# A fill and a wait on GpSimd after every gather of an edge-convolution kernel

## The chip, the cores and the metric

One core of a Trainium2 chip runs the whole kernel. The metric is the device time of one execution in microseconds. Three runs of the kernel before took 2430.92, 2434.01 and 2440.19 us; the median is 2434.01 us.

## The reference

A graph has 6250 nodes with 64 features and 200,000 edges, sorted by their destination. What is computed, cut to what matters:

```
xn   = batch-normalised x (over the nodes, gamma, beta)
feat = concat(xn[dst], xn[src] - xn[dst])          # 200000 x 128
h    = relu(feat @ W1 + b1)                        # 200000 x 128
msg  = h @ W2 + b2                                 # 200000 x 64
agg  = segment_max(msg, dst, 6250), 0 where a node has no edge
out  = layernorm(x + relu(agg))                    # over the 64 features
```

## The kernel before

The first layer is split: one part of it depends on the destination node alone, the other on the source node alone. So the kernel first makes two tables in DRAM, `a_dram` (destination part) and `b_dram` (source part, one row of 128 floats for every node). The edges are cut into two halves (h = 0, 1) and these into windows; the main loop runs over 196 steps (`NI`), k = 0 to 195, each with four tiles of 128 edges from either half, 1024 edges in all.

A step gets the source part of its edges in one of three ways.

- 28 steps (`picked`, every seventh) take it by matmuls with one-hot tiles: DVE makes the one-hot tiles (line 919, `oh`), PE multiplies them (lines 1146 and 1153, `ps_g`). This work is spread over all steps.
- The first 12 gathered steps (`gather(g)`, line 494) have rows of `x` fetched, 64 floats each, into `xs`, a view of `xb`.
- The other 156 (`gather_wide(i)`, line 511) have rows of `b_dram` fetched into `xb[:, u]`, one of eight buffers (`NXB`). PE transposes them straight into the hidden layer's bank (line 1205, `rows_wide`).

A gather is one indirect DMA that POOL issues: its index column `src_ix[:, b, q + t, h:h + 1]` names 128 rows, one for every partition. A step takes 8 gathers (4 tiles, 2 halves; the very first step takes 4). There are 92 narrow and 1248 wide ones, 1340 in all.

POOL's program is in order and short: it makes constants (lines 478 to 486), issues the 12 narrow groups, loads a flag, waits until `b_dram` is written, issues the 156 wide groups, and at the end scatters the last rows of the output (line 526). What paces it in the wide groups is the reuse of the eight buffers. Group i from 8 on waits until PE has transposed group i - 8:

```
                if i >= NXB:
                    pool.wait_ge(wide_ps, i - NXB + 1)
                elif i >= NXB - NX // 2:
                    pool.wait_ge(x_ps, 2 * u + 2)
```

On the other side PE waits in `rows_wide` on `wide_in[u]`, which the landed gathers raise. Nothing else waits for POOL in the main loop. In each step PE does, in order: the transposes of the running maxima of step k - 2 (`turn`, line 1196), the hidden layer of step k (lines 1205 and 1215), the messages of step k - 1 (line 1190), the node sums of step k - 2 (line 1234) and its share of one-hot matmuls. ACT takes `ps_mr` and the hidden layer out of PSUM (lines 683, 688) and makes the window's one-hot rows (lines 640, 644). DVE makes the pick masks (line 972), scans the messages (line 993) and makes `oh`. Once in seven windows DVE and ACT also do a layer norm (lines 923 to 954). SP loads keys, resets, tables and node windows on a queue of its own.

Of the kernel before, what the change touches and what calls it, by code (L numbers as in the profile page):

```python
# [6 lines left out]
def edge_conv_program(nc, x, src, dst, gamma, beta, W1, b1, W2, b2, out):  # L7
# [13 lines left out]
    P = 128  # L21
    N, C = x.shape
# [65 lines left out]
    def wide_slot(i):  # L88
        return (i + NX // 2) % NXB
# [4 lines left out]
    def sides(k):  # L94
        return 1 if k == 0 else 2

    def landed(g):
        return 16 * TG * sides(gathered[g])
# [11 lines left out]
    with ctx:  # L110
        def sb(name, shape, dt=f32):
            return ctx.enter_context(nc.sbuf_tensor(name, shape, dt))
# [4 lines left out]
        def sem(name):  # L117
            return ctx.enter_context(nc.semaphore(name))
# [65 lines left out]
        col_row = sb("col_row", [1, P], i32)  # L184
        msg = sb("msg", [C1, P])
        acc = sb("acc", [P, C1])
        xblk = sb("xblk", [P, C])
        cen_sq = sb("cen_sq", [P, C])
        nrm = sb("nrm", [P, 5])
        yblk = sb("yblk", [P, C])  # L190

        src_tv = src_t[:, :].rearrange("p (h b e) -> p h b e", h=2, b=NB)
        src_b = src_t[0:PN, 0:2 * GE]
# [22 lines left out]
        step = step_t[0:NW, :, :]  # L216
        sums = step_t[:, :, :].rearrange("p h e -> p (h e)")[0:ROWS, 0:WB * C].rearrange("p (w c) -> p w c", c=C)
        res, cen = part[:, :], part_sq[:, :]
        xt = best[:, 0:TH * PN]
        xt_v = xt.rearrange("p (q e) -> p q e", e=PN)  # L220
        fold = best[:, TH * PN:TH * PN + P]
# [68 lines left out]
        acc_ps, added = sem("acc_ps"), sem("added")  # L290
        end_step, end_sq, end_std, xwin_used = sem("end_step"), sem("end_sq"), sem("end_std"), sem("xwin_used")
        y_ready, y_out, tail_out = sem("y_ready"), sem("y_out"), sem("tail_out")

        g_in, g_pair_in, g_x_ps, g_x_sb = sem("g_in"), sem("g_pair_in"), sem("g_x_ps"), sem("g_x_sb")
        g_hid_ps, g_hid_sb, g_msg_ps, g_msg = sem("g_hid_ps"), sem("g_hid_sb"), sem("g_msg_ps"), sem("g_msg")
# [18 lines left out]
        def edge_tiles(eng, body):  # L314
            with eng.Fori(0, E // P) as i:
                body(i, i * P)
            if E % P:
                body(E // P, E - P)

        @block.sync  # L320
        def _(sp):
# [74 lines left out]
            def starts(ap, last):  # L396
                _, firsts = nc.values_load_multi_w_load_instructions(
                    ap, engines=[mybir.EngineType.SP], min_val=0, max_val=last,
                    skip_runtime_bounds_check_because="in_order is set only where every start lies in 0..last")
                return firsts  # L400
# [75 lines left out]
        @block.gpsimd  # L476
        def _(pool):
            pool.memset(ident[:, :], 0.0).then_inc(consts_ready, 1)
            pool.wait_ge(consts_ready, 1)
            pool.affine_select(out=ident[:, :], in_=ident[:, :], compare_op=ALU.not_equal, fill=1.0, base=0,  # L480
                               pattern=[[-1, P]], channel_multiplier=1).then_inc(consts_ready, 1)
            pool.iota(slot_row[:, :], pattern=[[1, SL]], base=1, channel_multiplier=0,
                      allow_small_or_imprecise_dtypes=True).then_inc(consts_ready, 1)
            pool.iota(slot_rep[:, :], pattern=[[1, SL], [0, NPC]], base=1, channel_multiplier=0,
                      allow_small_or_imprecise_dtypes=True).then_inc(consts_ready, 1)
            pool.iota(part_col[:, :], pattern=[[0, 1]], base=0, channel_multiplier=1,
                      allow_small_or_imprecise_dtypes=True).then_inc(consts_ready, 1)

            def gather(g):
                k = gathered[g]  # L490
                b, q = divmod(k * TG, SB)
                for t in range(TG):
                    for h in range(sides(k)):
                        pool.indirect_dma_start(xs[:, g, t, h, :], None, x[:, :],  # L494
                                                bass.IndirectOffsetOnAxis(ap=src_ix[:, b, q + t, h:h + 1], axis=0))\
                            .then_inc(rows_in[g], 16)

            def gather_wide(i):
                k = gathered[NX + i]
                u = wide_slot(i)  # L500
                if i == 0:
                    pool.wait_ge(b_first, 32)
                    pool.wait_ge(b_out, 32 * (AG - 1))
# [4 lines that stand above are left out]
                b, q = divmod(k * TG, SB)  # L508
                for t in range(TG):
                    for h in range(2):  # L510
                        pool.indirect_dma_start(xb[:, u, t, h, :], None, b_dram[:, :],  # L511
                                                bass.IndirectOffsetOnAxis(ap=src_ix[:, b, q + t, h:h + 1], axis=0))\
                            .then_inc(wide_in[u], 16)

            pool.wait_ge(src_ix_ready, 2)
            for g in range(NX):
                gather(g)
            pool.wait_ge(flag_ready, 1)
            windowed = pool.value_load(in_order[0:1, 0:1], min_val=0, max_val=1)
            with pool.If(windowed == 1):  # L520
                pool.wait_ge(src_ix_ready, 5)
                for i in range(len(gathered) - NX):
                    gather_wide(i)

                def scatter(p):
                    pool.indirect_dma_start(out[:, :], bass.IndirectOffsetOnAxis(ap=tail_ix[0:ROWS, p:p + 1], axis=0),
                                            y[:, p, :], None, bounds_check=N - 1, oob_is_err=False).then_inc(tail_out, 16)

                pool.wait_ge(tail_ready, 1)
                pool.wait_ge(y_ready, LB // WB + 1)  # L530
                pool.wait_ge(y_out, 32 * LB)
                for p in range(WB - 2):
                    scatter(p)
                for p in range(WB - 2, WB):
                    pool.wait_ge(y_ready, len(GROUPS) - WB + p + 1)
                    scatter(p)
            with pool.Else():
                for u in range(NX):
                    pool.wait_ge(rows_in[u], landed(u))

                def edge_tile(i, first):
                    loaded = pool.to_reg(i * 48 + 48)
                    pool.wait_ge(src_ix_ready, 2)
                    pool.wait_ge(g_in, loaded)
                    for side in range(2):
                        pool.indirect_dma_start(pair[:, side, :], None, x[:, :],
                                                bass.IndirectOffsetOnAxis(ap=pair_ix[:, side:side + 1], axis=0)).then_inc(g_pair_in, 16)

                edge_tiles(pool, edge_tile)
# [787 lines left out]
```

## Time and profile before

| | |
|---|---|
| median of three runs | 2434.01 us (2430.92 to 2440.19) |
| span of the profiled execution, first to last instruction | 2422.7 us |
| time of the profiled execution itself | the page gives the span alone; the median of the runs is 11.3 us above the span |
| PE busy (matmul records) | 1818.5 us, 75% |
| DVE, POOL, ACT busy | 1292.7, 1283.2, 862.0 us (53%, 53%, 36%) |
| mean granted clock of TensorE | 0.878 of full |

A busy share is the share of the span in which an engine had an instruction at work. The ends of the PE records are modelled, so PE can be fuller than its share says. The releaser "remote" stands where the profile names no instruction that ended just then.

### The profile page before, as it was taken

The numbers are of one execution on the slowest core, as the hardware profiler recorded it, in microseconds if no ns is written. First come the engines' busy times: TensorE is split into PE (matmuls) and PEld (weight loads), VectorE is DVE, ScalarE is ACT, GpSimd is POOL, SyncE is SP. The second block draws the span as 40 slices with busy tenths as digits, with TensorE's granted clock in tenths as the row PEclk, the third lists the DMA queues.
The fourth block names the chain that finished last, engine by engine and source line by source line (L and its number), as shares of the span: only waits on it lengthen the run. The fifth ranks groups of instructions, "written<-read, shape, count | busy, mean of one in ns | idle before, by whom it ended". The sixth has DMA issues, their size and how long they took to land.

```text
span 2422.7 us, 31826 instructions
## 1 busy us (share of the span) xinstructions
PE 1818.5 (75%) x12305; PEld 938.5 (39%) x12305; DVE 1292.7 (53%) x2070; ACT 862.0 (36%) x968; POOL 1283.2 (53%) x1356
## 2 busy tenths in 40 slices
PE   2046887787878778787878878878788778887785
PEld 1032444343434434343434444444444434444443
DVE  2054655565555555555555556556456555565553
ACT  2044443333333333333333333333334333333333
POOL 7715245556555565456555565555655565555621
PEclk6557899998999999898989899998999988898996
DMA  4154223233333332333323333233323333333320
GB/s 93 35 173 122 59 84 81 77 90 86 80 86 84 88 95 70 85 81 96 87 70 91 87 87 80 81 89 95 89 72 94 91 81 81 75 94 87 76 62 5
DMA packets 132832, 202.31 MB, mean 84 GB/s; under 512 B 74828, under 2 KB 76937, under 8 KB 132648
## 3 DMA queue, kind: packets, MB, share of 16 engines
q0 software_dynamic: 43440, 85.03, 16.5%
q1 hardware_dynamic: 87946, 115.04, 14.9%
q8 instruction: 97, 1.59, 0.3%
q10 hardware_dynamic: 1294, 0.20, 0.1%
q14 instruction: 55, 0.45, 0.1%
HBM read 189.19 MB, written 12.60 MB: 83 GB/s over the span
## 4 chain that ended last, share of the span: by engine, by line
another core or an unknown queue 38%; PE 29%; ACT 19%; issue 8%; DVE 5%; DMA 1%; SPq 0%; POOLq 0%; DVEq 0%; ACTq 0%
PE ps_g L1146 10%; PE ps_g L1153 6%; ACT hid L688 5%; ACT best L640 5%; PE ps_mr L1190 4%; ACT best L644 4%; ACT best L683 3%; PE ps_acc L1234 2%; DVE oh L919 2%; PE ps_h L1205 2%; PE ps_mr L1196 2%; PE ps_h L1215 1%; DVE runmax L993 1%; PE ps_h L1222 1%
## 5 line engine op out<-in xcount | busy, mean ns | idle before, releaser
L511 POOL DMA_INDIRECT xb<-b_dram,src_ix x1248 | 1181.1, 946 | 1031.4 <-PE ps_h L1205 384.9
L919 DVE TENSOR_SCALAR oh<-ps_k 128x1024 bf16<-128x1024 bf16 x1372 | 849.6, 678 | 1.0
L1146 PE MATMUL ps_g<-oh,xtab 128*128 128x512 bf16 x2744 | 643.5, 387 | 5.8 <-issue 5.0
L1190 PE MATMUL ps_mr<-hid,w 128*64 128x512 f32 x784 | 270.8, 776 | 369.9 <-ACT best L683 325.6
L972 DVE TENSOR_TENSOR best<-ps_acc,last_key 128x336 f32<-128x336 f32 x196 | 99.3, 507 | 815.8 <-remote 655.9
L683 ACT ACTIVATE best<-ps_mr 128x512 f32<-128x512 f32 x196 | 117.0, 597 | 1097.1 <-remote 816.3
L1146 PEld LDWEIGHTS ps_g<-oh,xtab 128*128 128x128 bf16 x2744 | 256.9, 99 | 375.6 <-issue 103.3
L1153 PE MATMUL ps_g<-oh,xtab 128*64 128x512 bf16 x2744 | 387.1, 424 | 12.6 <-issue 11.3
L993 DVE TENSOR_TENSOR_SCAN runmax<-rb,runmax,ps_mr 128x512 f32<-128x512 bf16 x196 | 249.6, 1274 | 97.4 <-PE ps_mr L1190 55.1
L688 ACT ACTIVATE hid<-ps_h,bias 128x1024 f32<-128x1024 f32 x196 | 217.9, 1112 | 106.8 <-remote 42.2
L1190 PEld LDWEIGHTS ps_mr<-hid,w 128*64 128x64 f32 x784 | 44.1, 154 | 479.6 <-ACT best L683 391.8
L1153 PEld LDWEIGHTS ps_g<-oh,xtab 128*64 128x64 bf16 x2744 | 168.0, 124 | 156.9 <-issue 68.2
L644 ACT ACTIVATE best<-best,ones 126x1024 bf16<-126x1024 bf16 x196 | 225.1, 1148 | 6.4
L640 ACT ACTIVATE best<-kb,minus_key 126x1024 bf16<-126x1024 bf16 x196 | 224.2, 1144 | 0.0
L1234 PEld LDWEIGHTS ps_acc<-best 128*42 128x42 f32 x3136 | 150.3, 148 | 163.4 <-issue 152.1
L1205 PE MATMUL ps_h<-ident,xb 128*128 128x128 f32 x1248 | 172.3, 277 | 25.2 <-issue 24.9
L1234 PE MATMUL ps_acc<-best 128*42 128x65 f32 x3136 | 159.2, 258 | 1.9 <-DVE best L972 1.1
L1205 PEld LDWEIGHTS ps_h<-ident,xb 128*128 128x128 f32 x1248 | 144.1, 142 | 29.5 <-issue 29.3
L1196 PE MATMUL ps_mr<-ident,runmax 128*128 128x128 f32 x784 | 122.7, 279 | 9.2 <-DVE runmax L993 7.1
L1215 PE MATMUL ps_h<-best,aw 126*128 126x512 bf16 x392 | 123.0, 392 | 8.6 <-issue 7.3
L1196 PEld LDWEIGHTS ps_mr<-ident,runmax 128*128 128x128 f32 x784 | 97.2, 143 | 56.5 <-issue 17.2
L494 POOL DMA_INDIRECT xb<-in_x,src_ix x92 | 89.3, 971 | 30.5 <-issue 27.7
(181 smaller groups left out, 537.2 us busy)
## 6 DMA issues: line engine op xcount, KB each, us to landing
kb<-keys_dram SPq DMA_DIRECT2D x98, 504.0 KB
rb<-reset_dram SPq DMA_DIRECT2D x98, 256.0 KB
xb<-b_dram,src_ix POOLq DMA_INDIRECT x1248
src_t<-in_src SPq DMA_DIRECT2D x56, 256.0 KB
aw<-a_dram SPq DMA_DIRECT2D x196, 31.5 KB
a_dram<-oh SPq DMA_DIRECT2D x6, 672.0 KB, 3.5
xwin<-xp_dram SPq DMA_DIRECT2D x196, 10.5 KB
out<-y SPq DMA_DIRECT2D x182, 10.5 KB
```

What stands on the lines that cost most here:

```text
L511: pool.indirect_dma_start(xb[:, u, t, h, :], None, b_dram[:, :], bass.IndirectOffsetOnAxis(ap=src_ix[:, b, q + t, h:h + 1], axis=0))\
L640: act.activation(onehot[:, k % 2, :, :], kb[0:SR, s, :].rearrange("p (h e) -> p h e", h=2)[:, :, i * GE:(i + 1) * GE], ACT.Abs, bias=minus ...
L644: act.activation(onehot[:, k % 2, :, :], onehot[:, k % 2, :, :], ACT.Relu, bias=ones[0:SR, 0:1], scale=-1.0).then_inc(onehot_ready, 1)
L688: act.activation(hid[:, k % 2, :, :], ps_h[:, :, :], ACT.Relu, bias=bias1[:, :]).then_inc(hid_sb, 1)
L919: dve.tensor_scalar(oh[0:PN, n % NOH, :], node_keys_ps, n % TN + 0.5, None, ALU.is_equal).then_inc(oh_ready, 1)
L993: dve.tensor_tensor_scan(runmax[:, (k - 1) % 2, :], rb[:, s, i * GE:(i + 1) * GE], ps_mr[:, :], runmax[:, k % 2, GE - 1:GE], ALU.add, ALU. ...
L1146: last = pe.matmul(ps_g[:, h, :], xtab[0:PN, t, 0:2, :].rearrange("p w c -> p (w c)"), oh[0:PN, n % NOH, h * GE:(h + 1) * GE], start=t == ...
L1153: pe.matmul(ps_g[h * C:(h + 1) * C, h, :], xtab[0:PN, n % TN, 2, :], oh[0:PN, n % NOH, h * GE:(h + 1) * GE], start=False, stop=False)
L1190: last = pe.matmul(ps_mr[h * C:(h + 1) * C, :], w2[:, :], hid[:, j % 2, h, :], start=True, stop=True)
L1196: last = pe.transpose(ps_mr[:, t * P:(t + 1) * P], runmax[:, j % 2, t * P:(t + 1) * P], ident[:, :])
L1205: last = pe.matmul(ps_h[:, h, t * P:(t + 1) * P], xb[:, u, t, h, :], ident[:, :], is_transpose=True, start=t == 0, stop=False)
L1234: last = pe.matmul(ps_acc[h * 64:h * 64 + SL, p * C1:(p + 1) * C1], pick[:, j % 2, t * 2 + h, :], rows[:, j % 2, t * 2 + h, :], start=(i = ...
```

## The change

After every gather, narrow or wide, POOL fills a scratch tile of 128 partitions and 192 float columns with zeros, has the fill raise the new semaphore `spaced`, and waits for the new value before it goes on. The gather itself is not waited for: its landing raises `rows_in` or `wide_in` as before. The scratch tile takes the place of three tiles of 64 columns (`xblk`, `cen_sq`, `yblk`) that only the branch for unordered inputs uses; they become views of it, so the memory taken stays the same. That branch isn't run here.

```
-        xblk = sb("xblk", [P, C])
-        cen_sq = sb("cen_sq", [P, C])
+        spacer = sb("spacer", [P, 3 * C])
         nrm = sb("nrm", [P, 5])
-        yblk = sb("yblk", [P, C])
...
+        xblk, cen_sq, yblk = spacer[:, 0:C], spacer[:, C:2 * C], spacer[:, 2 * C:3 * C]
...
+        spaced = sem("spaced")
...
+            handshakes = [0]
+
+            def space():
+                pool.memset(spacer[:, :], 0.0).then_inc(spaced, 1)
+                handshakes[0] += 1
+                pool.wait_ge(spaced, handshakes[0])
+
             def gather(g):
...
                             .then_inc(rows_in[g], 16)
+                        space()
...
             def gather_wide(i):
...
                             .then_inc(wide_in[u], 16)
+                        space()
```

## Rows read from the trace of the kernel before

**Rows 1.** The page: busy time and share of each engine, and POOL's slices.
```profile
PE 1818.5 (75%) x12305; PEld 938.5 (39%) x12305; DVE 1292.7 (53%) x2070; ACT 862.0 (36%) x968; POOL 1283.2 (53%) x1356
...
POOL 7715245556555565456555565555655565555621
```

**Rows 2.** The longest waits: engine, line, releaser: us, times, longest.
```profile
ACT best L683 <- remote: 816.3, 120, 8.5
DVE best L972 <- remote: 655.9, 124, 8.1
PEld ps_mr L1190 <- ACT best L683: 391.8, 126, 7.9
POOL xb L511 <- PE ps_h L1205: 384.9, 52, 17.8
```

**Rows 3.** Line 1205 (PE, both records): what ended the idle time before it.
```profile
its engine sat idle before it (us, times) until:
  issue: 54.2, 75
```

**Rows 4.** POOL in order of time, a group amid the loop: start, us, what.
```profile
1027.19 0.94 POOL L511 DMA_INDIRECT xb<-b_dram,src_ix  x1 [1.62 <-remote]
1028.43 0.94 POOL L511 DMA_INDIRECT xb<-b_dram,src_ix  x1 [0.30 <-issue]
...
1038.94 0.94 POOL L511 DMA_INDIRECT xb<-b_dram,src_ix  x1 [2.06 <-PE ps_h L1205]
```

**Rows 5.** POOL's groups: instructions | busy us, mean ns | idle before, releasers.
```profile
L478 POOL MEMSET ident<- 128x128 f32 x1 | 0.2, 204 | 0.3 <-POOLq L1327 0.3
L1327 POOL MEMSET const-float32-0.0<- 128x1 f32 x1 | 0.1, 98 | 0.3 <-issue 0.3
```

**Rows 6.** POOL, the first gathers of wide groups 8 and 155.
```profile
330.90 0.94 POOL L511 DMA_INDIRECT xb<-b_dram,src_ix  x1 [12.39 <-PE ps_h L1205]
...
2325.20 0.98 POOL L511 DMA_INDIRECT xb<-b_dram,src_ix  x1 [15.95 <-PE ps_h L1205]
```

**Rows 7.** Line 511 in the loop: window, length, POOL busy (x), granted clock, DMA.
```profile
330.00:2337.00 2007.00, 1120.52 (x1184) 0.91 0.32 85
```

**Rows 8.** PE, the transposes of the last wide group (155).
```profile
2401.48 1.97 PE L1205 MATMUL ps_h<-ident,xb 128*128 128x128 f32 x8
```

**Rows 9.** DMA issues: KB where known, median us from issue to landing.
```profile
out<-y,tail_ix POOLq DMA_INDIRECT x7, 3.4
```

**Rows 10.** In order of time, the first us: POOL, and DVE line 773.
```profile
0.75 0.20 POOL L478 MEMSET ident<- 128x128 f32 x1 [0.29 <-POOLq L1327]
...
1.20 0.28 POOL L480 TENSOR_SCALAR_AFFINE_SELECT ident<-ident 128x128 f32<-128x128 f32 x1 [0.25 <-POOL ident L478]
1.45 0.17 POOL L482 IOTA slot_row<- 128x42 f32 x1
...
4.64 0.46 DVE L773 CAST src_ix<-ps_h 128x8 int32<-128x8 f32 x2 [0.51 <-PE ps_h L1059]
...
5.38 1.13 POOL L494 DMA_INDIRECT xb<-in_x,src_ix  x1 [2.79 <-DVE src_ix L773]
```

**Rows 11.** POOL, the last narrow gather and the first wide one.
```profile
121.51 0.94 POOL L494 DMA_INDIRECT xb<-in_x,src_ix  x1 [0.30 <-issue]
173.64 0.95 POOL L511 DMA_INDIRECT xb<-b_dram,src_ix  x1 [51.19 <-DMA b_dram<-xb]
```

**Rows 12.** DVE and POOL beside each other in a layer norm and before it.
```profile
1017.64 1.27 DVE L919 TENSOR_SCALAR oh<-ps_k 128x1024 bf16<-128x1024 bf16 x2
1017.84 0.94 POOL L511 DMA_INDIRECT xb<-b_dram,src_ix  x1 [0.30 <-issue]
...
1021.63 0.62 DVE L941 TENSOR_TENSOR bias<-step_t,norm 106x448 f32<-106x448 f32 x1
1021.75 1.32 POOL L511 DMA_INDIRECT xb<-b_dram,src_ix  x1 [0.30 <-issue]
```

**Rows 13.** Line 1146, PE: duration ns, least, median, most.
```profile
L1146 PE MATMUL ps_g<-oh,xtab x2744: 376/379/634, 216.0 to 2362.6; 128*128 128x512 bf16 x196
```

## The prediction

> **What bounds the kernel now.** I read the page's busy times first. PE is the fullest engine by its records, POOL and DVE stand at 53%, and POOL's slices are flat at 5 or 6 tenths over the whole loop [rows 1]. Then the waits [rows 2]: ACT's line 683 and DVE's line 972 both wait for `turn_ps`, which PE raises, and PE's own line 1190 waits for ACT's 683. So the steps go around the ring PE, ACT, PE. The releaser "remote" of ACT and DVE is, by the code, PE as well, whose ends are modelled too early. POOL is not in that ring: it waits 384.9 us for PE's line 1205, and in the other direction before the transposes of the gathered rows PE's idle time was ended by no DMA, only by 54.2 us of "issue" [rows 3]. POOL follows PE, and PE never waits for a gather.
>
> How far ahead POOL is can be read from its order of time. Eight gathers take 8 x 1.25 = 10.0 us (a record of 0.94 and a gap of 0.30), and the next group starts 11.75 us after this one, since it must wait for a buffer that PE frees once a step [rows 4]. Every seventh step is a picked one that frees nothing, and POOL stands still for 12 to 18 us [rows 2, 6]. Over the loop that gives 147 group periods from 330.90 to 2325.20, which is 13.57 us for a group, or 1.696 us for a gather [rows 6]. POOL needs 1.25. It refills a buffer that PE reads again only eight groups later.
>
> **The room, worked out.** Suppose POOL never waits again after group 8's start at 330.90. Group 155 must have landed when PE reads it at 2401.48 [rows 8]. The only gather-like transfer with a landing time is the final scatter, 3.4 us [rows 9]; I take that. 148 groups are 1184 gathers [rows 7]: (2401.48 - 3.4 - 330.90) / 1184 = 1.746 us. Up to 1.696 us for a gather POOL still waits for PE at times; from 1.696 to 1.746 it eats the lead of eight groups; above 1.746 each further 0.01 us costs 11.8 us of kernel time. The room is 1.746 - 1.248 = 0.498 us per gather.
>
> **What a fill with its wait adds.** Three terms.
> - The fill itself. A memset of 128 columns took 204 ns and one of a single column 98 ns [rows 5], so a column costs 106/127 = 0.83 ns, and 192 columns 98 + 191 x 0.83 = 0.257 us.
> - The way back into the next gather. Where a gather follows a wait, it starts 0.28 us after the releaser's end (DVE's line 773 ends at 5.10, the gather starts at 5.38) and where a POOL operation waits for POOL's own memset, 0.25 us after it [rows 10]. This takes the place of the 0.30 us that a gather starts after a gather today [rows 4]. Net -0.02 to -0.05; I take -0.02.
> - The way from the gather into the fill, which no row shows. From below it is 0: line 482 starts right behind line 480, with no wait between them [rows 10]. From above it is the 0.30 us of a gather behind a gather. But of those 0.30 us a gather pays 0.28 also behind a wait, when POOL has long been empty; so they belong to the start of a gather, and the one before it leaves 0.02 to 0.05. I take 0.05.
>
> The sum is 0.257 - 0.02 + 0.05 = 0.29 us, and a gather comes to 1.54 us. The ends: from below 0.257 - 0.05 = 0.21 us, or less if most of the fill runs beside the gather, down to nothing (1.25 us); from above 0.257 - 0.02 + 0.30 = 0.54 us (1.79 us). The first end is inside the room of 0.498 us, the last is 0.04 outside it.
>
> At 1.54 us a group takes 12.3 us. In a run of six wide steps POOL falls back 0.5 us a group behind PE's 11.8, some 3 us in all, and gets it back in the picked step. It stays nearly the whole lead ahead: group 155 still starts at 2325.20, when its buffer comes free, and has landed at 2325.2 + 12.3 + 3.4 = 2340.9, 60 us before 2401.48. So 1184 x 0.29 = 343 us of new POOL time lie in 1184 x 0.45 = 530 us in which POOL waited for PE. Busy POOL rises by 1340 x 0.257 = 344 us, the span by nothing.
>
> **The stretches around the loop.** The 92 narrow gathers end at 122.45 and POOL then waits 51.19 us for `b_dram` [rows 11]. 92 x 0.29 = 27 us fit; the cover is gone only at (173.64 - 5.38) / 92 = 1.83 us a gather. Their readers come later than that in PE's program, behind both tables. The wide groups 0 to 2 then take 3 x 8 x 1.54 = 37.0 us, to 210.6, and group 3 waits for a buffer until about 211.6 anyway. Behind POOL's new wait stands only the next gather, whose sole reader is PE; SP, ACT and DVE get nothing from POOL in the loop, and the final scatters start after more than 60 us of idle time. The memory map keeps its size, so I cost the views at nothing.
>
> **A rule weighed.** A gather whose time falls beside DVE's line 941, with two SBUF inputs, took 1.32 instead of 0.94 us, while gathers beside DVE's line 919, which reads PSUM, keep 0.94 [rows 12]. The Trainium skill, "SBUF — State Buffer", section on who interferes with whom, says that a two-input DVE instruction contends with a GpSimd instruction that reads SBUF and not with one that only writes, and that DVE's modes with two ports lock GpSimd out; line 919 would be outside both by its PSUM input. The trace agrees for the gathers. By that rule the fill stands in nobody's way and the sum stays at 1.54. A second rule speaks against the sum: the Trainium skill, "Perfetto Trace Analysis", GPSIMD instruction and SWDGE parts, holds that a gather's record ends with the last descriptor and not with the end of the instruction on the DSPs, so the fill may start later than the record's end. By it the third term would be anything up to 0.30, the rival below.
>
> **Rivals.**
> - POOL becomes the bound (slower). The fill starts a full 0.30 us after a gather's record, as the next gather does today, and a gather takes 1.79 us: (1.79 - 1.746) x 1184 = 52 us, 2486 us. It decides from 1.746 us on, with PE's line 1205 waiting for landings in the last third of the loop. For it: the gap is there after every gather and no row shows a memset there. Against it: the same gap follows an empty engine. A larger form: DVE's line 919 holds up the fills. It is busy 1372 x 0.68 = 933 us by its records' length, about 0.37 of the loop, with a mean rest of 0.34 us, so 0.13 us for each fill. Alone that gives 1.67, inside the room; with the 0.30 us gap it gives 1.92 us and 1184 x 0.17 = 206 us, 2640 us. Chance of the first 0.12, of the second or anything near it 0.06.
> - The clock changes its pattern (either side). PE's matmul takes 379 ns as a rule and 634 ns at the lower level [rows 13]; the granted clock is 0.91 in the loop [rows 7], that is some 0.18 of its 2007 us at 1.2 GHz. The loop then loses some 0.09 x 2007 = 180 us of PE work to that level. Other arrival times of rows could shift this by a tenth: 18 us either way, 2416 or 2452 us. Nothing in the profile ties it to POOL, whose groups PE gets far ahead. Chance 0.09 faster, 0.05 slower.
> - The change doesn't space anything: the fill runs on idle parts of POOL beside the gather's work and the wait is met at once. Gathers keep about 1.25 us; the time is that of before. Chance 0.06.
>
> **The numbers.** The forecast proper, 1.54 us a gather and no change of time, has 0.62. With the last rival, no change has 0.68. Slower has 0.12 + 0.06 + 0.05 = 0.23, faster 0.09. A measurement here can tell about 0.5%, 12 us. The sums are made on the profiled execution; its span of 2422.7 us lies 11.3 us under the median of the runs, and since the sum is zero the forecast is that median, 2434 us. The forecast's own range is 2426 to 2442. The range for 8 in 10 goes up to 2490, to take in POOL as a mild bound, and down to 2420; the large form of that rival and the far part of a faster clock are left out.
>
> **What would show it.** Right: POOL's gathers start 1.45 to 1.65 us apart within a group; memsets of about 0.26 us between them; POOL's idle time until line 1205 shrinks by about 300 us but is not gone; group starts still 13.6 us apart on average; line 1205 with no DMA among its releasers. Wrong: a spacing over 1.75 us, POOL back to back from 330 us to the end, and line 1205 waiting for `xb` from some point on. If the spacing is as said and the time moves all the same, then PE's ring or its clock has changed and my claim that POOL is outside the ring fails.

## The result and the profile after

The changed kernel took 2196.81 us (median of four, 2191.44 to 2214.6) against 2433.34 us for the kernel before beside it: a ratio of 0.9031 with a 95% interval of 0.9000 to 0.9062. The forecast was no change, and the time lies far outside its range. The profiled execution took 2195.2 us, with a span of 2193.2 us.

The page of the changed kernel: span, busy times, POOL's slices, and the two groups of instructions that the change touches. Lines of this kernel are eight or nine higher than before (511 is 519 now, 683 is 692, 972 is 981, 1196 is 1205, 1205 is 1214).

```profile
span 2193.2 us, 33134 instructions
PE 1742.0 (79%) x12117; PEld 921.5 (42%) x12305; DVE 1295.1 (59%) x2070; ACT 872.8 (40%) x968; POOL 1660.7 (76%) x2696
...
POOL 7877778888887768777788688876878788877842
...
L519 POOL DMA_INDIRECT xb<-b_dram,src_ix x1248 | 1189.6, 953 | 433.6 <-issue 252.6
...
L492 POOL MEMSET spacer<- 128x192 f32 x1340 | 365.8, 273 | 1.6
```

POOL has 365.8 us of fills more (344 were forecast), its share goes from 53% [rows 1] to 76%, and the whole is 229.5 us of span shorter. The longest waits of the changed kernel, in the form of [rows 2]:

```profile
ACT best L692 <- remote: 583.8, 85, 14.6
DVE best L981 <- remote: 502.4, 92, 11.8
...
ACT best L692 <- PE ps_mr L1205: 267.8, 65, 7.7
```

The waits "remote" of ACT and DVE fell from 120 and 124 times [rows 2] to 85 and 92. (Their sums, 816.3 to 583.8 us for ACT, hold the idle time that ACT has in any step too, 3.8 us as shown below.) Two stretches share the gain. The first transposes of running maxima in each kernel, as one line of each (duration, first and last start):

```profile
L1196 PE MATMUL ps_mr<-ident,runmax x784: 269/273/476, 209.4 to 2409.6; 128*128 128x128 f32 x196
```
```profile
L1205 PE MATMUL ps_mr<-ident,runmax x784: 269/273/476, 95.7 to 2180.0; 128*128 128x128 f32 x196
```

The first of these is the kernel before. Its loop on PE begins 113.7 us later than the changed kernel's, and takes 115.9 us longer (2200.2 against 2084.3). POOL gives another cut of the same 229.5 us: the wide gathers start at 173.6 before and at 149.6 after; from the first to the last of them it is 2160.4 us before and 1962.1 after; the tail behind them 88.7 and 81.5. So by POOL's cut 24 us come from the start, 198 from the stream of wide gathers, and 7 from the tail. Both cuts say only where in the run the time went; what the fills of each stretch are worth is measured by g2 below.

### What the "remote" waits are

In the kernel before I put PE's matmuls, ACT and POOL of one stretch side by side. First PE, then ACT, then POOL; start, length, line, and in brackets the idle time before it.

```profile
1013.60 0.60 PE L1196 MATMUL ps_mr<-ident,runmax 128*128 128x128 f32 x4
...
1022.74 0.60 PE L1196 MATMUL ps_mr<-ident,runmax 128*128 128x128 f32 x4
...
1035.74 0.60 PE L1196 MATMUL ps_mr<-ident,runmax 128*128 128x128 f32 x4
1036.17 1.04 PE L1205 MATMUL ps_h<-ident,xb 128*128 128x128 f32 x8
1037.05 0.60 PE L1215 MATMUL ps_h<-best,aw 126*128 126x512 bf16 x2
```
```profile
1014.24 0.60 ACT L683 ACTIVATE best<-ps_mr 128x512 f32<-128x512 f32 x1 [4.50 <-PE ps_mr L1196]
1015.54 1.11 ACT L688 ACTIVATE hid<-ps_h,bias 128x1024 f32<-128x1024 f32 x1 [0.71 <-PE ps_h L1215]
...
1026.86 0.60 ACT L683 ACTIVATE best<-ps_mr 128x512 f32<-128x512 f32 x1 [4.00 <-remote]
1027.36 1.11 ACT L688 ACTIVATE hid<-ps_h,bias 128x1024 f32<-128x1024 f32 x1
...
1038.62 0.60 ACT L683 ACTIVATE best<-ps_mr 128x512 f32<-128x512 f32 x1 [6.71 <-remote]
1039.11 1.11 ACT L688 ACTIVATE hid<-ps_h,bias 128x1024 f32<-128x1024 f32 x1
```
```profile
1015.35 0.94 POOL L511 DMA_INDIRECT xb<-b_dram,src_ix  x1 [17.79 <-PE ps_h L1205]
...
1024.63 0.94 POOL L511 DMA_INDIRECT xb<-b_dram,src_ix  x1 [0.30 <-issue]
...
1035.94 0.95 POOL L511 DMA_INDIRECT xb<-b_dram,src_ix  x1 [0.30 <-issue]
```

The transposes that end at 1014.20 fall while POOL stands still: ACT starts 0.04 us later, and its next instruction waits 0.71 us for the hidden layer, which is PE's true pace. Those that end at 1023.34 fall amid gathers: ACT starts 3.52 us later, 1.29 us after the last gather's end, and its next instruction waits for nothing. Those of 1036.34: 2.28 us later, 1.73 us after the last gather. A record's end modelled too early would be too early at 1014.20 too. It isn't. So PE had finished, and its completion signal was seen late. The signal records say the same: in the last case the three signals `turn_ps`, `wide_ps` and `hid_ps` were seen at 1038.59, 1038.69 and 1038.73, within 0.14 us, although the work that raises them ends at 1036.34, 1037.21 and 1037.64. Counted from these records over the loop, `turn_ps` comes more than 0.15 us late in 145 of 196 steps, by 3.49 us in the median of the 145 and by 502 us in sum.

Signal records are not complete in every run, so from here on I count lateness by instructions: `turn_ps` is late at ACT when line 683 starts over 0.15 us after both the end of PE's record and the end of ACT's own instruction before it. In the kernel before that is so in 131 steps, 411 us in sum. With POOL idle when the signal falls due (no gather running or ended less than 0.6 us ago) it is late in 3 of 54 steps, amid gathers in 128 of 142. And in 122 of the 131 it is seen only when POOL's gathers have stopped, in the median 1.73 us after the last of them ended. The signals that go the other way, from ACT's line 683 and DVE's lines 919 and 993 to PE, let PE start at most 1.6 us after they are due, and at most 0.95 us in the trace of f2 below, where nothing is late.

POOL's own wait for `wide_ps` is among the held signals. So a group of gathers holds back the signal that starts the next group: in the group of [rows 4], 8 x 1.25 of gathers and 1.75 until it is seen is 11.75 us, the very step that I had read as PE's work. PE's work for such a step is 8.5 us. Here is ACT in the changed kernel where nothing is held:

```profile
1013.25 0.60 ACT L692 ACTIVATE best<-ps_mr 128x512 f32<-128x512 f32 x1 [3.83 <-PE ps_mr L1205]
...
1021.74 0.60 ACT L692 ACTIVATE best<-ps_mr 128x512 f32<-128x512 f32 x1 [3.85 <-issue]
```

### The profile page after: what moved, and what is told of

The parts are those of the page before. It is cut to its first block, busy times and chain, and to the rows that moved or that the text cites. A ratio compares the mean times of both kernels' runs of the same rounds, so it can differ in the third digit from the quotient of the medians.

```text
span 2193.2 us, 33134 instructions
## 1 busy us (share of the span) xinstructions
PE 1742.0 (79%) x12117; PEld 921.5 (42%) x12305; DVE 1295.1 (59%) x2070; ACT 872.8 (40%) x968; POOL 1660.7 (76%) x2696
## 4 chain that ended last, share of the span: by engine, by line
PE 52%; another core or an unknown queue 19%; ACT 11%; issue 10%; DVE 6%; SPq 1%; DMA 0%; ACTq 0%; POOL 0%; DVEq 0%; POOLq 0%
PE ps_g L1155 18%; PE ps_g L1162 10%; PE ps_mr L1199 8%; PE ps_h L1214 4%; PE ps_acc L1243 3%; PE ps_mr L1205 3%; ACT hid L697 3%; DVE oh L928 3%; ACT best L649 2%; ACT best L653 2%; PE ps_h L1224 2%; ACT best L692 2%; PE ps_h L1231 1%; DVE runmax L1002 1%
## 5 line engine op out<-in xcount | busy, mean ns | idle before, releaser
L1155 PE MATMUL ps_g<-oh,xtab 128*128 128x512 bf16 x2556 | 596.0, 383 | 30.4 <-issue 28.4
L1199 PE MATMUL ps_mr<-hid,w 128*64 128x512 f32 x784 | 257.7, 741 | 341.4 <-issue 225.8
L692 ACT ACTIVATE best<-ps_mr 128x512 f32<-128x512 f32 x196 | 116.9, 597 | 906.8 <-remote 583.8
L1162 PE MATMUL ps_g<-oh,xtab 128*64 128x512 bf16 x2744 | 375.8, 418 | 1.8 <-issue 0.9
L492 POOL MEMSET spacer<- 128x192 f32 x1340 | 365.8, 273 | 1.6
L1243 PEld LDWEIGHTS ps_acc<-best 128*42 128x42 f32 x3136 | 143.2, 141 | 153.3 <-issue 142.2
L1243 PE MATMUL ps_acc<-best 128*42 128x65 f32 x3136 | 151.6, 250 | 1.9 <-DVE best L981 1.1
```

The lines of the kernel that those rows point to most:

```text
L492: pool.memset(spacer[:, :], 0.0).then_inc(spaced, 1)
L1155: last = pe.matmul(ps_g[:, h, :], xtab[0:PN, t, 0:2, :].rearrange("p w c -> p (w c)"), oh[0:PN, n % NOH, h * GE:(h + 1) * GE], start=t == ...
L1162: pe.matmul(ps_g[h * C:(h + 1) * C, h, :], xtab[0:PN, n % TN, 2, :], oh[0:PN, n % NOH, h * GE:(h + 1) * GE], start=False, stop=False)
L1199: last = pe.matmul(ps_mr[h * C:(h + 1) * C, :], w2[:, :], hid[:, j % 2, h, :], start=True, stop=True)
L1243: last = pe.matmul(ps_acc[h * 64:h * 64 + SL, p * C1:(p + 1) * C1], pick[:, j % 2, t * 2 + h, :], rows[:, j % 2, t * 2 + h, :], start=(i = ...
```

## The experiments

Two kinds of condition turned up, by chip, and every run has the kernel before beside it on the same chip. On chips 0, 1, 7 and 9 the kernel before takes 1713 to 1717 us. On chips 6, 14 and 15 it takes 2439 to 2446, as it did where it was first measured (2433). I call the first kind "signals in time" and the second "signals late"; the comparison below of two profiles of the same kernel is the reason for the names. Each chip was used in one stretch of time only, so that the chip decides, and not the moment, is likely but not shown.

### On chips with signals in time

**e1, h1.** The kernel before with only the first eight wide groups gathered. The other 148 groups are left out, and PE, which waits for these eight alone, reads their rows again, so the output is wrong:

```
-                for i in range(len(gathered) - NX):
+                for i in range(NXB):
...
-                    pe.wait_ge(wide_in[u], wide_landed(i))
+                    pe.wait_ge(wide_in[u], wide_landed(i % NXB))
```

> The kernel before, but only the first eight wide groups are gathered; PE reads their rows again for the other 148 groups and waits only for the first filling of a buffer, so most source rows are wrong data. Theory H (held signals): in the kernel before, a completion signal of PE that falls due after the third gather of a group, issued back to back, is seen by ACT, DVE and POOL only after the group's last gather has landed; a wide step then lasts 8 x 1.25 + 1.75 = 11.75 us, whatever PE has to do. Without gathers no signal is late, a wide step takes the 8.5 us that undisturbed steps show in both traces, and the whole takes about 1850 to 2000 us, below the changed kernel's 2197. Rival P (PE is full at 11.75 us of real work a step, its records being modelled too short): no more than a few per cent below 2434.

> The kernel with only the first eight wide groups gathered, again (its output is that of stale rows). On chips where the kernel before takes 1714 us it took 1718. If the kernel before takes about 2434 here: theory H (gathers hold PE's signals) says the loop runs as on the other chips, and only the narrow gathers still cost their part of the start, so 1800 to 1900 us. Rival K (this kind of chip has slower PE signals or slower PE whatever POOL does): well over 2100 us. If the kernel before takes 1714 us here: 1718 again.

Measured: 1717.59 us beside 1713.82 (ratio 1.0017, 1.0007 to 1.0027), and again 1716.20 beside 1717.27 (0.9997, 0.9985 to 1.001). Where signals are in time, the gathers cost PE nothing at all. What the loop would take without gathers where signals are late stays untried.

**e2, h2.** The fills moved: none after a single gather of a wide group, four with their waits after the eighth. **e3, h3, i2.** A fill after every gather, but three scratch tiles, and a wait only for the fill three back. **e4, h4, i1, j2.** The fill cut to one column, the wait kept.

```
+                    for n in range(4):      # e2, behind the two loops of a group
+                        space()
...
+                if handshakes[0] >= 3:      # e3
+                    pool.wait_ge(spaced, handshakes[0] - 2)
+                pool.memset(spacer[:, handshakes[0] % 3, :], 0.0).then_inc(spaced, 1)
...
+                pool.memset(spacer[:, 0:1], 0.0).then_inc(spaced, 1)      # e4
```

> The changed kernel with the eight fills and waits of a wide group replaced by four at the group's end: the eight gathers go back to back (1.25 us apart) and POOL then pauses for four fills with their waits, 4 x 0.54 = 2.2 us, so a group takes as long on POOL as in the changed kernel, 12 us. Theory H: the stream of eight holds PE's signals as before, and the pause ends it: a step takes 10 + about 2.2, so the time is that of before or up to 4% more, 2430 to 2530. Rival S (what counts is how many gathers there are per us on average, which eases the DMA engines and memory): same mean rate as the changed kernel, so about 2200.

> Four fills with waits after each wide group, one after every narrow gather, again; 1964 us on a chip where the kernel before took 1714. If the kernel before takes about 2434 here: theory H says that a stream of eight holds the signals to its end, a step takes 10 + about 2 us, and the start gains about 56 us, so 2380 to 2450 us. Rival S (mean rate of gathers): 2200, as the changed kernel.

> The changed kernel with three scratch tiles in turn, where POOL waits for the fill three gathers back instead of the last one, so that its queue is never empty: fills stay between the gathers, the round trip goes. Gathers 1.50 us apart or a little less. Theory H with the break made by the fill (time between gathers): 2200 as the changed kernel. Theory H with the break made by the empty queue (the sequencer waits for a signal and nothing is queued): PE's signals stay held to the group's end, a step takes 8 x 1.5 + 1.75 = 13.75 us, and the time rises above the one of before, to 2500 to 2750. Rival S: 2200.

> Fills between the gathers but a wait that lags by three, again; 1900 us on a chip where the kernel before took 1714. If the kernel before takes about 2434 here: if a break needs POOL's queue to run empty, PE's signals are held as in the kernel before, through fills of 0.27 us and all, and a step takes 8 x 1.39 + 1.75 = 12.9 us, so 2500 to 2600 us; if the time between two gathers counts, 2150 to 2250 us.

> Fills between the gathers, a wait that lags by three. If the kernel before takes about 2434 here: if a break needs POOL's queue to run empty, PE's signals are held through fills of 0.27 us and all, and a step takes 8 x 1.39 + 1.75 = 12.9 us, so 2500 to 2600 us; if only the time between two gathers counts (0.44 us here), 2150 to 2300 us. If the kernel before takes 1714 here: 1900.

> The changed kernel with a fill of one column instead of 192, the wait kept: gathers about 1.35 us apart (0.94 + 0.1 + 0.27 and some). Theory H with the break made by the wait: signals get through as in the changed kernel or better, and POOL needs 8 x 1.35 = 10.8 us a group instead of 12.0, so 2050 to 2200 us. Theory H with the break made by a pause of enough length: between 2200 and 2430. Rival S: between 2200 and 2430 as well, near 2330.

> A fill of one column and the wait after every gather, again; 1843 us on a chip where the kernel before took 1714. If the kernel before takes about 2434 here: if an empty queue is what breaks the hold, 2050 to 2150 us, below the changed kernel's 2197, since a group takes 10.6 us of POOL instead of 12.0; if the length of the pause counts, above 2197.

> A fill of one column and the wait after every gather. If the kernel before takes about 2434 here: where any pause after every gather lets PE's signals through, 2050 to 2150 us, below the changed kernel's 2197, since a group takes 10.6 us of POOL instead of 12.0; where the length of the pause counts (0.38 us between two records instead of 0.55), above 2197 and up to 2434. If the kernel before takes 1714 here: 1840.

Measured, all slower than before: e2 1963.80 us (ratio 1.1457, 1.1438 to 1.1476), h2 1961.40 (1.1428, 1.14 to 1.1456); e3 1900.44 (1.1092, 1.1073 to 1.111), h3 1900.68 (1.1069), i2 1898.51 (1.1072); e4 1842.67 (1.0755, 1.0737 to 1.0772), h4 1839.11 (1.0717), i1 1840.55 (1.0729). They agree from chip to chip within 0.2%. The expectations of the e runs spoke of the other condition, so as tests of it they say nothing; for h1 to h4, i1 and i2 the branch for this condition only repeats what the e runs gave, and it came true. What these runs do show is that here a pause is paid in full: e4 and f1 (below) differ by 220 us, and 1340 gathers by 0.17 us are 228.

**f1, f2.** The changed kernel unaltered, and the kernel before with its profile kept, side by side.

> The changed kernel unaltered, to see what it does where the kernel before takes 1714 us. Theory C (two conditions of the chip): where PE's signals are not held up, PE takes about 8.5 us a wide step and the kernel before is bound by PE and by POOL nearly alike (1714 us); the changed kernel's POOL then needs 8 x 1.50 = 12.0 us a group, 156 groups are 1872 us, and with the start before them the time is 1990 to 2060 us, 16 to 20% slower than before. Where the kernel before takes about 2434 us, the ratio is 0.90 as first measured. Rival (the gain belongs to the changed kernel wherever it runs): faster than 1714.

> The kernel before unaltered, for its trace. Theory C: where it takes about 1714 us, PE's turn_ps is seen by ACT's line 683 within 0.1 us of the end of PE's record, at any place in POOL's group, the releaser is PE and not 'remote', and wide steps are 8.5 us apart; where it takes about 2434 us, the trace is that of the first. Rival: the same time lies elsewhere (a shorter select, faster DMA landings).

Measured: f1 2062.77 us beside 1715.78 (1.2015, 1.1992 to 1.2038), 3 us above the range that was expected; f2 1711.97. **The change that saves 10% on one chip costs 20% on another.** The kernel before on this chip: page and waits.

```profile
span 1709.9 us, 31638 instructions
PE 1600.8 (94%) x12117; PEld 874.0 (51%) x12305; DVE 1293.2 (76%) x2070; ACT 872.0 (51%) x968; POOL 1285.0 (75%) x1356
...
q0 software_dynamic: 43440, 85.03, 24.2%
...
PE 89%; ACT 3%; DVE 2%; issue 2%; SPq 2%; DMA 1%; ACTq 1%; POOLq 0%; DVEq 0%
...
L511 POOL DMA_INDIRECT xb<-b_dram,src_ix x1248 | 1181.9, 947 | 380.4 <-issue 378.3
...
L683 ACT ACTIVATE best<-ps_mr 128x512 f32<-128x512 f32 x196 | 116.8, 596 | 536.5 <-PE ps_mr L1196 529.4
```
```profile
L1196 PE MATMUL ps_mr<-ident,runmax x784: 270/273/477, 89.7 to 1696.8; 128*128 128x128 f32 x196
```
```profile
1012.49 0.60 ACT L683 ACTIVATE best<-ps_mr 128x512 f32<-128x512 f32 x1 [4.50 <-PE ps_mr L1196]
...
1020.98 0.60 ACT L683 ACTIVATE best<-ps_mr 128x512 f32<-128x512 f32 x1 [3.85 <-PE ps_mr L1196]
```

The instructions are the same, DVE's and ACT's busy times are equal to about 1%, a gather takes 947 ns and the transfers have the same bytes; there is no "remote" wait of ACT at all, the step is 8.49 us, and PE is 94% busy. `turn_ps` is late at ACT in none of 196 steps: line 683 starts within 0.04 us. POOL runs back to back: of its 380.4 us of idle time before line 511, 378.3 are the 0.30 gaps, so it has no room whatever. Both engines need about the whole loop. For the changed kernel (f1), the chain of waits and two of its rows:

```profile
POOL 79%; issue 18%; PE 2%; DMA 0%; DVE 0%; POOLq 0%; ACT 0%; DVEq 0%
```
```profile
POOL xb L519 <- POOL spacer L492: 336.3, 1228, 0.6
PE ps_h L1214 <- DMA xb<-b_dram,src_ix: 253.1, 61, 10.2
```

This is the rival "POOL becomes the bound", at 1.50 us a gather and not at the 1.75 that it named: POOL is back to back, and PE's line 1214 waits 253.1 us for landings. From the first wide gather to the last it is 1887.6 us, which is 1248 x 1.51.

### On chips with signals late

**g1, g2.** g1: no fill after narrow gathers, and one after every fourth wide gather. g2: fills after the 92 narrow gathers alone.

```
+                        if t % 2 == 1 and h == 1:      # g1, in gather_wide
+                            space()
```

> The changed kernel with the fill and its wait only after every fourth gather of the wide groups, and none after the narrow gathers. Theory C, where PE's signals come in time (kernel before near 1714 us): POOL is busy back to back in the kernel before, so each pause is paid: 156 x 2 x 0.25 = 78 us, 1760 to 1800 us. Where they come late (kernel before near 2434 us): a pause after four gathers lets signals through twice a group; if any pause does, 2000 to 2200 us, if a hold needs the stream to end, 2434 and above.

> The changed kernel with the fill and its wait only after the 92 narrow gathers. Theory C, where PE's signals come in time: POOL starts its wide groups 92 x 0.25 = 23 us later and is back to back from there, 1714 to 1740 us. Where they come late: the start gains what ACT's line 596 waited in the kernel before, up to 87 us, and the loop nothing: about 2350 us.

Measured beside 2443.73 us: g1 2522.15 (1.0316, 1.0256 to 1.0376), **slower** than no fill at all; g2 2387.61 (0.9779, 0.9734 to 0.9825). g2's stream of wide gathers takes 2152.0 us, as before (2160.4); its gain is the start: first transposes at 94.3 us instead of 209.4. So the fills of the start alone are worth 56 us, and those of the wide groups the rest: from g2's ratio of 0.978 to the change's 0.903. The expectation for g2 named this split, with 2350 us for it.

**j1, j2.** j1: fills after all narrow and after every second wide gather (`if h == 1: space()`). j2: the kernel of e4, one column after every gather.

> The changed kernel with the fill and its wait after every second gather of the wide groups (and after every narrow one). If the kernel before takes 1714 here: POOL pays 156 x 4 x 0.25 + 92 x 0.25 = 179 us, less what it is ahead, so 1870 to 1900 us. If the kernel before takes about 2434 here: after every gather gained 10% and after every fourth lost 3%; if signals get through wherever no more than two gathers stand back to back, 2050 to 2200 us, if only an empty queue after every gather does it, 2400 to 2500 us.

> A fill of one column and the wait after every gather. If the kernel before takes about 2434 here: where any pause after every gather lets PE's signals through, 2050 to 2150 us; where the length of the pause counts, 2197 to 2434 us. If the kernel before takes 1714 here: 1840.

Measured beside 2445.69 us: j1 2425.42 (0.9869, 0.9811 to 0.9927), j2 2508.86 (1.0236, 1.0179 to 1.0292). j2 tells two explanations apart. The rival was that POOL's wait after each gather is what helps, since it empties POOL's queue of issued work. j2 has all 1340 waits and loses 2.4%, against its expectation on either branch. So the wait by itself is not it; the time between gathers is.

**k1, k2.** The fill at 128 and at 384 columns (`spacer[:, 0:2 * C]`; `spacer = sb("spacer", [P, 6 * C])`).

> The changed kernel with a fill of 128 columns instead of 192: gathers about 1.44 us apart instead of 1.50. If the kernel before takes about 2440 here: with 1.33 us between starts a kernel took 2509 and with 1.50 us 2197, so somewhere between the signals begin to get through; if the spacing decides gradually, 2280 to 2380 us, if only 1.50 us or more does it, about 2450 to 2550. If the kernel before takes 1714 here, POOL's stream is the bound: 1840 + 1340 x (1.44 - 1.33) = 1990 us.

> The changed kernel with a fill of 384 columns: gathers about 1.66 us apart. If the kernel before takes about 2440 here: POOL alone needs 1340 x 1.66 and some, 2275 us; if all signals are in time at this spacing the time is that, 2270 to 2310, if they are still late, above 2310. If the kernel before takes 1714 here: 2275 us by POOL's stream.

Measured beside 2439.44 us: k1 2360.07 (0.9704, 0.9662 to 0.9746), k2 2280.26 (0.9354, 0.9338 to 0.9369). Both lie in a branch of their expectations: k1 in "gradually", k2 in "all signals in time". k2's page, chain and waits:

```profile
POOL 8888888888888888888888888888888888888886
...
POOL 81%; issue 16%; PE 1%; DMA 0%; DVE 0%; POOLq 0%; ACT 0%; DVEq 0%
...
L492 POOL MEMSET spacer<- 128x384 f32 x1340 | 579.7, 433 | 1.8
```
```profile
PE ps_h L1214 <- DMA xb<-b_dram,src_ix: 405.1, 89, 12.1
```

At 1.66 us no wait of ACT is put down to "remote", and `turn_ps` is late at ACT in none of 196 steps, on a chip where the kernel before takes 2439 us. POOL's own stream is the bound.

### All of them by the spacing of gathers

| kernel, signals late | start to start of wide gathers | first transposes at | stream of wide gathers | less 1248 x spacing | loop on PE | `turn_ps` late at ACT, of 196 | of these, seen amid gathers | ratio |
|---|---|---|---|---|---|---|---|---|
| before | 1.248 | 209.4 | 2160.4 | 603 | 2200 | 131 | 9 | 1 |
| g2, narrow spaced | 1.248 | 94.3 | 2152.0 | 595 | 2280 | 129 | 13 | 0.978 |
| g1, every fourth | 1.310 (mean) | 190.5 | 2275.2 | 640 | 2328 | 113 | 30 | 1.032 |
| j2, 1 column | 1.328 | 170.8 | 2280.7 | 623 | 2326 | 97 | 29 | 1.024 |
| j1, every second | 1.372 (mean) | 94.3 | 2199.8 | 487 | 2320 | 95 | 33 | 0.987 |
| k1, 128 columns | 1.443 | 112.8 | 2122.7 | 322 | 2216 | 92 | 55 | 0.970 |
| the change, 192 | 1.497 | 95.7 | 1962.1 | 94 | 2084 | 110 | 101 | 0.903 |
| k2, 384 columns | 1.657 | 92.9 | 2092.2 | 24 | 2172 | 0 | 0 | 0.935 |
| before, in time (f2) | 1.248 | 89.7 | 1561.0 | 4 | 1607 | 0 | 0 | |
| the change, in time (f1) | 1.497 | 91.7 | 1887.6 | 19 | 1956 | 0 | 0 | |

"Seen amid gathers" means that a gather is running, or ended less than 0.6 us ago, when ACT starts on the signal.

The fifth column is what POOL's stream takes beyond its own gathers and fills, so it is what POOL waits. It stays at about 600 us up to 1.33, falls to 322 at 1.44 and to 94 at 1.50. It is not the amount by which signals are late: part of its fall is POOL's own stream, which grows by 1248 x 0.25 = 312 us into the same waits. POOL's stream is the sum of this and the spacing, so the time first rises (g1, j2: the pauses are paid and little is gained), has its lowest tried point at 192 columns, and rises again.

What changes with the spacing is when a held signal gets through. At 1.25 us nearly all late ones wait until the gathers stop (122 of 131). At 1.33 us 29 of 97 are seen amid gathers, at 1.44 us 55 of 92, at 1.50 us 101 of 110, and at 1.66 us none is late. So at 192 columns most signals still come late, but they no longer need POOL to stand still. Their sum at ACT falls little: 411 us before, 475 in g2, 365 in the change. The hidden layer's signal `hid_ps` is even late more often in the change than before (121 steps against 12, 137 us against 42). How the 116 us that the loop gains add up from these stays open.

The third column shows the same for the narrow gathers. Until the wide gathers begin, at 144 to 174 us, nothing but the spacing of the 92 narrow ones differs between the kernels: 209.4 and 190.5 at 1.25 (these two differ by 19 us with the same narrow gathers), 170.8 at 1.33, 112.8 at 1.44, 94 to 96 at 1.50, 92.9 at 1.66, and 90 to 92 where signals are in time.

## Why the prediction was wrong, by its steps

**The step that failed** is in the first paragraph: "The releaser 'remote' of ACT and DVE is, by the code, PE as well, whose ends are modelled too early." The releaser is PE; its ends are not too early. ACT starts 0.04 us after them when POOL is idle, and in the stretch shown 2.28 and 3.52 us after them amid gathers. From the misreading came "POOL is not in that ring". POOL was in the ring through the time at which PE's signals are seen, and the 11.75 us step was POOL's own group time and not PE's work, which is 8.5 us a step.

A row that contradicts my reading was in the trace of before, and my prediction did not weigh it. ACT's copies of the tables, in the first 130 us, while POOL issues narrow gathers back to back until 122.45 [rows 11]:

```profile
82.11 0.60 ACT L596 ACTIVATE oh<-ps_x 128x512 bf16<-128x512 f32 x1 [41.05 <-remote]
...
130.41 0.60 ACT L596 ACTIVATE oh<-ps_k 128x512 bf16<-128x512 f32 x1 [46.34 <-remote]
```

The two signals for these copies fell due with PE's records at 42.13 and 45.96 and were recorded at 82.08 and 130.38, 40 and 84 us late; in the changed kernel they fell due at 28.93 and 30.77 and were recorded within 0.3 us. No modelled end is wrong by 40 us. The changed kernel has no such wait; g1, which leaves the narrow gathers unspaced, has `ACT oh L605 <- remote` with 89.8 us again, and g2 has none.

- *The room of 0.498 us per gather* was sound as arithmetic for a PE that comes as late as in [rows 8]. On chips with signals in time PE comes at 8.5 us a step, a group of gathers takes 10.0, and the room is nil: the 20% of f1. Where it was worked out it held: POOL's waits for PE before the wide gathers ("PE ps_h" and "remote") shrink from 580 us to 78 and are not gone, and PE never waits for a landing.
- *What a fill adds*: a fill took 273 ns where 257 was worked out, the gather behind it starts 0.27 us after it, and the fill itself starts at the end of the gather's record. 0.95 + 0.27 + 0.27 is 1.50 us per gather against a forecast of 1.54. The term taken as 0.05, with 0.30 as its upper end, is 0. The rule of the Trainium skill, "Perfetto Trace Analysis", SWDGE part, that a gather's record ends with the last descriptor and not with the end of the instruction on the DSPs, would have allowed a fill to start later than the record's end; the trace shows no such delay: all 1340 fills start within 0.02 us of it.
- *No interference from DVE*: right. 610 fills lie beside DVE's line 928, and none of them takes over 0.28 us. The rule of the Trainium skill, "SBUF — State Buffer", section on who interferes with whom, that a DVE instruction with two SBUF inputs contends with a GpSimd instruction that reads SBUF and not with one that only writes, holds for the fill as well: beside line 950 (line 941 before) the longest of 8 fills took 0.293 us, while 9 of the 11 wide gathers beside line 941 took over 1.1 us in the kernel before. One fill of the 1340 took 0.733 us, in the start, beside lines 819 and 820.
- *The narrow stretch*: 92 fills do lie under other work, but what they freed was worth 113.7 us of PE's start (56 us of the whole, by g2) and was not in the sum.
- *The clock rival*: the mean granted clock went from 0.878 to 0.907, and is 0.973 in f2, with PE busy 75%, 79% and 94%; a matmul of the message layer (line 1190) took 776 ns in the kernel before, 741 in the changed one and 624 in f2. So the clock differs too, and its part is in every difference of times here. An estimate of it from PE's busy time outside line 1146, of whose records some are missing in the changed kernel and in f2: 1175 us before, 1146 in the change, 1013 in f2, so some 30 of the 229.5 us that the change gains, and some 160 of the 713 us between the two conditions. That the clock moved by itself would not explain ACT starting late on a finished record.
- *The check that I named* did its work: the spacing is as said, the time moved all the same, and by the prediction's own last sentence the claim that POOL is outside the ring fails.

**Shown:** the late signals are PE's; they are late amid gathers (128 of 142) and seldom beside an idle POOL (3 of 54); at 1.25 us between gathers they mostly wait for the stream to stop, at 1.50 they get through in it, at 1.66 none is late; the wait for the fill without the spacing gains nothing (j2); and the change gains only where signals are late. **Argued only:** what holds them. The signal records suggest the landings. Each wide gather raises its semaphore 16 times; where signals are in time, 19,598 of 19,968 such raises are recorded, in the kernel before where they are late 5,629, as if the rest came in merged. That PE's signals share a path with these raises fits, but no run changed the number of raises for the same rows, and records are missing for a signal that is never late too: of ACT's own signal from line 640 to 644 the kernel before has 114 for 196 steps and f2 all of them, and line 644 starts within 0.04 us of it in both. **Open:** why chips 6, 14 and 15 differ from 0, 1, 7 and 9, or whether it is the chip at all; and how the loop's gain adds up. Also open is whether the gathers must be evenly spaced or only fewer in a microsecond on average; e2, with its pause after a group, and e3, with its lagging wait, would tell, but were not run where signals are late. By the table, e3 at 1.39 us should stand between j1 and k1; that is an estimate.

No kernel tried beats the others in both conditions: the kernel before is best where signals are in time (1714 us), the change where they are late (2197 us).

## What to carry to other kernels

Before the end of an engine's work is called the reason of a wait, check that the wait ends at that record's end in a stretch where the other engines are idle; "remote" with waits of tens of microseconds is not a modelling error. If a pause is meant to make room for something, sweep its length: 0.08 us per gather cost 2%, 0.19 us gained 3%, 0.25 us gained 10%, 0.41 us gained 6.5%. And time the kernel before on several chips before a fix for contention is kept: the same fix was worth -10% and +20%.

## What the runs showed of the hardware that was not expected

- One kernel, same instructions and transfers, takes 1712 us on some chips and 2434 on others (a factor of 1.42). Between repeats on one chip it moves by 0.5 to 0.8%.
- PE's completion signals can be seen 3 us late in the loop (median 3.2 us of the 131 late ones at ACT), and 40 and 84 us late in the start, while POOL issues indirect DMAs of 128 rows every 1.25 us; they then arrive together, three within 0.14 us. The first gathers of a burst do no harm yet: where at most three have begun, DVE starts on the messages' signal on time in 187 of 187 cases.
- How they get through depends on the rate: of the late signals 9 of 131 are seen amid gathers at one gather in 1.25 us, 55 of 92 at 1.44, 101 of 110 at 1.50, and none is late at 1.66.
- A POOL memset of 128 partitions by 1, 128, 192 and 384 float columns took 114, 220, 273 and 433 ns in place, and a gather starts 0.27 us after a wait for one.
